# The codebook search of a four-layer kernel: one fp32 matmul per unit in place of three bf16 matmuls

## The reference

```
d = jnp.sum(z_flat ** 2, axis=1, keepdims=True) + jnp.sum(codebook ** 2, axis=1) - 2.0 * jnp.matmul(z_flat, codebook.T)
idx = jnp.argmin(d, axis=1)
z_q = codebook[idx]
```

## Time and profile before

| engine | busy us (share of the span) | instructions |
|---|---|---|
| TensorE, matmuls | 1207.6 (73%) | 5997 |
| TensorE, weight loads | 747.5 (45%) | 6040 |
| VectorE | 1359.2 (82%) | 1885 |
| ScalarE | 430.0 (26%) | 1354 |
| GpSimd | 1009.7 (61%) | 977 |

### The profile page before, as it was taken

How to read it: one execution, slowest core, us unless ns; L and a number is a source line. 1 busy time by engine, 2 the same in 40 slices (tenths; PEclk the granted TensorE clock), 3 DMA queues, 4 the chain that set the end, 5 groups by cost and what they waited for, 6 DMA issues and landing times. The chain is left out here.

```text
span 1657.5 us, 19707 instructions
## 1 busy us (share of the span) xinstructions
PE 1207.6 (73%) x5997; PEld 747.5 (45%) x6040; DVE 1359.2 (82%) x1885; ACT 430.0 (26%) x1354; POOL 1009.7 (61%) x977
## 2 busy tenths in 40 slices
PE   5889989698889987689857685676665566555554
PEld 2455555354444444244336454544444444444443
DVE  5568678789999999989967889987887777797775
ACT  1241000124333443243457231221112212111111
POOL 6158578444333443235777677777777777777772
PEclk9889999899999999789978797697777778767677
DMA  4051000012111121053476796787877878777773
GB/s 168 13 166 40 1 0 0 15 31 58 53 43 34 46 58 39 20 153 107 142 225 201 216 288 208 211 267 229 247 209 228 248 229 247 211 232 212 208 210 99
DMA packets 111101, 232.64 MB, mean 140 GB/s; under 512 B 14676, under 2 KB 60500, under 8 KB 110748
## 3 DMA queue, kind: packets, MB, share of 16 engines
q0 software_dynamic: 58176, 191.30, 39.0%
q1 hardware_dynamic: 52828, 40.17, 7.7%
HBM read 205.15 MB, written 26.26 MB: 140 GB/s over the span
## 5 line engine op out<-in xcount | busy, mean ns | idle before, releaser
L2076 POOL DMA_INDIRECT code_region<-corners,lead_region x252 | 240.9, 956 | 77.9 <-issue 75.8
L1864 DVE SCALAR_TENSOR_TENSOR max_region<-score,nc,max_region 128x512 f32<-128x512 f32 x324 | 230.5, 740 | 28.4 <-PE score L1433 26.2
L742 POOL TENSOR_TENSOR prod_acc<-prod_acc,prod_pool 128x752 f32<-128x752 f32 (+8 forms) x112 | 151.8, 1355 | 98.1 <-DVE prod_pool L715 90.6
L2076 POOL DMA_INDIRECT early_region<-corners,lead_region x136 | 129.0, 948 | 41.3 <-issue 40.8
L1458 PE MATMUL score<-ident,code_region 128*128 128x128 f32 x540 | 96.9, 340 | 77.6 <-DVE code_region L1913 73.0
L2076 POOL DMA_INDIRECT max_region<-corners,lead_region x130 | 124.1, 955 | 39.6 <-issue 38.7
L2076 POOL DMA_INDIRECT late_region<-corners,lead_region x126 | 119.9, 951 | 44.6 <-issue 37.8
L1864 DVE SCALAR_TENSOR_TENSOR max_region<-lead_score,nc,max_region 128x512 f32<-128x512 f32 x180 | 132.2, 741 | 8.1 <-PE lead_score L1433 7.6
L1458 PEld LDWEIGHTS score<-ident,code_region 128*128 128x128 f32 x540 | 78.6, 176 | 94.8 <-DVE code_region L1913 87.5
L1991 POOL DMA_INDIRECT late_region<-code_rows,block_id x35 | 37.0, 1058 | 135.3 <-DVE block_id L1706 98.7
L664 PE MATMUL y_ps<-prod_pe,w_scale 128*128 128x384 f32 (+9 forms) x396 | 107.6, 397 | 0.0
(11 more groups left out here) (289 smaller groups left out, 3098.2 us busy)
## 6 DMA issues: line engine op xcount, KB each, us to landing
corners<-lead_region SPq DMA_DIRECT2D x72, 192.0 KB
corners<-lead_region SPq DMA_DIRECT2D x8, 576.0 KB
code_rows<-codes_n SPq DMA_DIRECT2D x8, 516.0 KB, 4.2
codes_t<-in_codes_t SPq DMA_DIRECT2D x8, 512.0 KB, 3.7
codes_n<-in_codes SPq DMA_DIRECT2D x8, 512.0 KB, 4.4
code_region<-corners,lead_region POOLq DMA_INDIRECT x252, 3.7
x<-in_x SPq DMA_DIRECT2D x2, 1152.0 KB, 6.3
out<-x SPq DMA_DIRECT2D x4, 576.0 KB, 3.3
```

What stands on the lines that cost most here:

```text
L742: pool.tensor_tensor(to, to, v, ALU.add).then_inc(pooled, 1)
L1864: dve.scalar_tensor_tensor(r, score[SLOT[k]], nc2[:, m:m + 1], r, ALU.add, ALU.max).then_inc(dve_took, 1)
L2076: pool.indirect_dma_start(quad(T, k), None, table[j].rearrange("n s c -> n (s c)"), bass.IndirectOffsetOnAxis(index[j % B][:, at:at + 1], 0))\
```

## The change

The codes are loaded as they are into the 8192 words, with no slots, and no waits between the loads; POOL no longer works on them. z is kept in fp32 alone. A unit is one fp32 matmul. `code_views` gives the eight groups one after another.

```diff
         def _(pool):
             opening.pool(pool)
-            beside.pool(pool)
...
-                         Opening(tools, parts, x, xpad, gm32, moments, loads), CodeSplit(nc, tools, parts, a, ch, cl))
+                         Opening(tools, parts, x, xpad, gm32, moments, loads), CodeLoad(tools, parts, a, codes_t))
...
-        dve.sem_inc(self.affine, 1)
-        chain(dve.tensor_scalar(z, first, scale[:, 0:1], self.first_shift[:, 0:1], ALU.mult, ALU.add))
-        dve.wait_ge(self.high, 1)
-        dve.tensor_tensor(zl, z, zh, ALU.subtract).then_inc(self.low, 1)
+        dve.tensor_scalar(z, first, scale[:, 0:1], self.first_shift[:, 0:1], ALU.mult, ALU.add).then_inc(self.first, 1)
...
-        pe.wait_ge(self.high, 1)
-        pe.wait_ge(self.low, 1)
+        pe.wait_ge(self.first, 1)
...
-        act.wait_ge(self.affine, 1)
-        act.activation(zh, self.x[:, 0:self.FIRST], ACT.Identity, bias=self.first_shift[:, 0:1],
-                       scale=self.scale[:, 0:1]).then_inc(self.high, 1)
...
-        pool.wait_ge(self.high, 1)
+        pool.wait_ge(self.first, 1)
...
         for a, c, b in cuts:
-            z, zh, zl = places(a, c)
-            pool.tensor_scalar(z, x[:, a:c], self.scale[:, b:b + 1], self.shift[:, b:b + 1], ALU.mult, ALU.add)\
+            pool.tensor_scalar(places(a, c), x[:, a:c], self.scale[:, b:b + 1], self.shift[:, b:b + 1], ALU.mult, ALU.add)\
                 .then_inc(rest, 1)
-        pool.wait_ge(rest, 6)
-        for a, c, b in cuts:
-            z, zh, zl = places(a, c)
-            pool.tensor_copy(zh, z).then_inc(rest, 1)
-        pool.wait_ge(rest, 9)
-        for a, c, b in cuts:
-            z, zh, zl = places(a, c)
-            pool.tensor_tensor(zl, z, zh, ALU.subtract).then_inc(rest, 1)
-
-    DONE = 12
+    DONE = 6
...
+class CodeLoad:
+    def __init__(self, tools, ctx, a, codes):
+        self.a, self.codes = a, codes
+        self.loaded = tools.sem(ctx, "codes_t_loaded")
+
     def sp(self, sp):
         for g in range(GROUPS):
-            s = g % self.SLOTS
-            if g >= self.SLOTS:
-                sp.wait_ge(self.low, g - self.SLOTS + 1)
-            sp.dma_start(self.ct[:, s, :], self.a["codes_t"][:, g, :]).then_inc(self.ct_in[s], 16)
-
-    def pool(self, pool):
-        for g in range(GROUPS):
-            s = g % self.SLOTS
-            pool.wait_ge(self.ct_in[s], 16 * (g // self.SLOTS + 1))
-            pool.tensor_copy(self.ch[g], self.ct[:, s, :]).then_inc(self.high, 1)
-            pool.wait_ge(self.high, g + 1)
-            pool.tensor_tensor(self.cl[g], self.ct[:, s, :], self.ch[g], ALU.subtract).then_inc(self.low, 1)
+            sp.dma_start(self.codes[:, g, :], self.a["codes_t"][:, g, :]).then_inc(self.loaded, 16)
+        sp.wait_ge(self.loaded, 16 * GROUPS)
...
 def code_views(region):
-    high, low = [], []
...
-    return high, low
+    return region[:, 0:CODES].rearrange("p (g n) -> p g n", g=GROUPS)
...
-                    high, low_ = chunk_of(zh_early, zh_late, n), chunk_of(zl_early, zl_late, n)
-                    pe.matmul(o, ch[g][:, w], high, start=True, stop=False)
-                    pe.matmul(o, ch[g][:, w], low_, start=False, stop=False)
-                    pe.matmul(o, cl[g][:, w], high, start=False, stop=True).then_inc(score_ready, 1)
+                    pe.matmul(o, codes_t[:, g, w], chunk_of(z_early, z_late, n), start=True, stop=True)\
+                        .then_inc(score_ready, 1)
```

More of the change, by code:

```diff
@@ L777, in layer0 @@
                      (gb[:], a["gamma_beta"])]
[L778 removed]
+            codes_t, nc2, code_rows = codes
             with ExitStack() as parts:
                 guidance(nc, tools, xpad, w_guide, ident, ident_b[:], (sel_a, id3a), (sel_b, id3b), wta, wtb,
[L781 removed]
+                         Opening(tools, parts, x, xpad, gm32, moments, loads), CodeLoad(tools, parts, a, codes_t))
             with ExitStack() as parts:
@@ L818, in __init__ @@
         self.group_rooted = tools.sem(ctx, "x_group_rooted")
-        self.affine = tools.sem(ctx, "z_affine")
-        self.high = tools.sem(ctx, "first_high")
-        self.low = tools.sem(ctx, "first_low")
+        self.first = tools.sem(ctx, "first_ready")
         self.shifts = tools.sem(ctx, "z_shifts")
@@ L833, in dve_early, with dve @@
         chain(dve.tensor_tensor(var_x, qx, var_x, ALU.subtract))
-    def dve(self, dve, ps, each, z, zh, zl):
+    def dve(self, dve, ps, each, z):
         chain = Chain(dve, self.step)
@@ L1083, in finale @@
     region_code, region_lead, region_early, region_max, region_late = places
[L1084 to L1087, removed]
+    codes_t = code_views(region_code)
+    z_early = region_early[:, 0:PX * EARLY]
     x_flat = x.rearrange("p b n -> p (b n)")
@@ L1094, in z_places @@
         if c <= EARLY * PX:
-            return [v[:, a:c] for v in (z_early, zh_early, zl_early)]
-        return [v[:, a - EARLY * PX:c - EARLY * PX] for v in (z_late, zh_late, zl_late)]
+            return z_early[:, a:c]
+        return z_late[:, a - EARLY * PX:c - EARLY * PX]
     with ExitStack() as ctx:
@@ L1686, in _ @@
             act.sem_inc(y_saved, 1)
-            between.act(act, zh_early[:, 0:PX])
+            between.act(act)
             search_steps(step)
@@ L1969, in _ @@
             dve.sem_inc(pos_ready, 1)
-            between.dve(dve, gps[:, 0:2 * B], y0[:, 0:2 * CH], z_early[:, 0:PX], zh_early[:, 0:PX], zl_early[:, 0:PX])
+            between.dve(dve, gps[:, 0:2 * B], y0[:, 0:2 * CH], z_early[:, 0:PX])
             search_steps(step)
@@ L2169, in program @@
         code_rows = nc.dram_tensor("code_rows", [CODES // PER, PER * ROW], F32).ap()
-        ch, cl = code_views(code_region[:])
+        codes_t = code_views(code_region[:])
         y = lead_region[:, 0:N]
         between = Between(tools, ctx, x.rearrange("p b n -> p (b n)"), y, stats, xy, moments, gb, gm32)
-        layer0(nc, tools, a, x, xpad, gm32, gm8, ident, (ch, cl, nc2, code_rows), y, stats, xy, moments, gb, between)
+        layer0(nc, tools, a, x, xpad, gm32, gm8, ident, (codes_t, nc2, code_rows), y, stats, xy, moments, gb, between)
         early_region = tools.sb(ctx, "early_region", [P, 5120])
```

10 lines of the change are left out of this document (1 added, 9 removed).

## The result

The changed kernel takes 1738.94 us, the median of 4 runs (1734.21 to 1739.90); the kernel before, beside it on the same chip, 1658.30. The ratio is 1.048, 95% interval [1.0468, 1.0493]. The profiled execution took 1738.93 us, with a span of 1737.1 us, 79.6 more than before. The forecast was 1733 (1712 to 1757).

What follows compares the result with a forecast made beforehand. TensorE was taken as the bound in all chunks but 6, which VectorE sets. 83.5 for the search - 6.5 - 1.0 - 1.7 = +74.3 us on 1659.3, less 1.3 to the runs' median, gave 1733 us (1712 to 1757).

Steps and rivals of the forecast that it cites:

- guidance: Stage before the search: without POOL's code splits, TensorE's first softmax wait and slow work behind it go; -6.5 us (-3.8 to -8).
- between the layers, to ScalarE's first unit: Before the search: TensorE starts on z itself, not on the result of VectorE's subtraction; -1.0 us.
- chunks 1 to 5: Codebook search: TensorE's 59.3 us plus 1.2 us of remaining wait make 60.5 per chunk, +9.4 each, +47 us for five.
- chunk 6: Search chunk with depthwise taps: TensorE leads until unit 10 of the first step, then VectorE's unchanged work; +3.5 us (0 to 13.5).
- chunk 7: Search chunk where the norm chain holds TensorE in the first step; four steps estimated together at +9 us (3 to 13.5).
- chunk 8: Last search chunk: TensorE is the bound except in step 1; +10.5 us (7 to 13.5).
- behind the search, to POOL's stream: End of search: POOL's gathers hang on the find at unit 7, so start less late than the search ends; -1.7 us (-4 to 0).
- from there to the end: From POOL's stream of gathers to the kernel's end: no change predicted, 0.
- The price of a unit: Search on TensorE: one fp32 matmul is two passes, 0.858 us instead of 0.647, 0.211 us more per unit.
- the first (less shows, +40 to +52): Rival, chance 0.07: VectorE's own work fills chunks 7 and 8 and step 1's slack holds; 1700 to 1711 us.
- The second: Rival, chance 0.05: fp32 matmul costs two bf16 matmuls, 0.432 us per unit, so VectorE sets each chunk; -34, 1626 us.
- the third: Rival, chance 0.06: weight loads or the clock show, 0.2 to 0.4 us more per unit; 1850 to 1960 us, partly from 1757.

## Why the prediction was right

| term | predicted | measured |
|---|---|---|
| guidance | -6.5 | -6.15 (branches begin at 79.29, before at 85.44) |
| between the layers, to ScalarE's first unit | -1.0 | -0.3 |
| chunk 0 | +13.5 | +14.0 |
| chunks 1 to 5 | +47 | +48.9 (60.88 against 51.1) |
| chunk 6 | +3.5 | +2.4 |
| chunk 7 | +9 | +7.8 |
| chunk 8 | +10.5 | +11.6 |
| behind the search, to POOL's stream | -1.7 | -2.3 |
| from there to the end | 0 | +3.7 |
| sum | +74.3 | +79.6 |

**The price of a unit** was read off and the earlier trace rows, from another fp32 matmul in the same kernel: two passes per call, each as long per column as two bf16 matmuls. It came out at 0.86 us, as predicted, and the run with four bf16 matmuls, with chunks of the same length, shows that TensorE pays for nothing else there.

**Who sets the pace.** TensorE in chunks 0 to 5, with little left of the waits for VectorE's find pairs in step 1. Here the count of VectorE's work between two uses of a bank was what mattered: 0.211 us times 64 units would have been 13.5 a chunk, and 9.8 came. TensorE's own work is the 59.3 us worked out (steps 0 and 3 with three turns 15.05 each, steps 1 and 2 with two 14.61 each); the rest, 1.56 us where 1.2 was predicted, lies at the unit named, unit 0 of step 2, and at the two pairs behind it:

```profile
642.55 2.78 PE L1389 MATMUL score<-late_region,code_region 128*128 128x512 f32 x6
646.44 1.99 PE L1389 MATMUL lead_score<-late_region,code_region 128*128 128x512 f32 x4 [1.11 <-DVE max_region L1821]
648.29 1.98 PE L1389 MATMUL score<-late_region,code_region 128*128 128x512 f32 x4
```

Three units from 642.55 would end at 645.12, the next begins at 646.44 (1.3 us); it and the three behind it take 1.85 and 1.83 us a pair instead of 1.72. The trace before has five such waits around this step in chunk 5 (586.72 to 598.47), not four, and the last two stand at units 0 and 2 of step 2, so the 5.3 us were not all in step 1.

**Chunks 6 to 8** came out near their sums, in part by luck. VectorE does set chunk 6: it is busy for 71.8 us of it (71.6 before). But the first step grew by 2.8 us where 2.1 was worked out, the next two by 1.2 and 1.0, and the last shrank by 2.6 (18.70 against 21.31), which the prediction doesn't have. With 256 columns the same chunk grew by only 0.8 (76.65 us), as its step 1 lost less to TensorE's lower clock level (last section). The steps of chunk 7 grew by 2.4, 2.5, 1.1 and 1.9 where 2.5, 1.6, 3.1 and 1.8 were estimated, those of chunk 8 by 3.4, 2.2, 3.1 and 2.9 where 3.4, 2, 1.7 and 3.4 were.

**Guidance.** The wait, the slow convolution behind it and the slow transposes went, as worked out, and all of it belongs to POOL's splitting: the run with the splits spread has the bf16 search and gained 6.3 us on the whole time. How well the size of this term was hit says little: where the splits stayed as they were, the branches begin at 83.19 us (four bf16 matmuls), 85.44 (before) and 85.66 (two).

**Between the layers** TensorE did start on z, 0.9 us earlier against the branches' start, but its first units are slow (TensorE in order of time, and the stage table of the first two units):

```profile
311.95 3.78 PE L1389 MATMUL lead_score<-early_region,code_region 128*128 128x512 f32 x4 [2.98 <-DVE early_region L882]
315.52 2.44 PE L1389 MATMUL score<-early_region,code_region 128*128 128x512 f32 x4
```

```profile
311.95:315.52 3.57, 3.57 (x4) 1.51 (x5) 0.01 (x1) 0.69 (x1) 3.02 (x2) 0.50 0.01 2
```

The first two units take 3.57 us (311.95 to 315.52), 1.79 each, twice 0.858 and a little more, at a granted clock of 0.50: this is the lower level, 1.2 GHz, behind a wait of 2.98 us. The kernel before starts at this level too (its first matmuls are 0.43 us apart, 319.82 to 320.25), but a unit is 1.28 us there. So the longer unit makes this start dearer: from TensorE's first unit to ScalarE's it is 2.1 us instead of some 1.5 (the trace before lacks the record of the first matmul; its start is put one spacing ahead of the second, at 318.97), which ate 0.6 here, and the first step of chunk 0 grew by 3.83 us where 16 x 0.211 = 3.4 would have been the price, which is the 0.5 by which chunk 0 missed. The term itself is small beside its spread: from the branches' start to ScalarE's first unit it is 232.4 to 235.6 us in the six kernels with bf16 matmuls.

**The largest miss** is the part of "behind the search" that should have stayed as it was: 3.7 us, of which 3.3 come behind the gather that waits over 6 us for TensorE (at 1004.19 us; before, at 927.87). The gathers that POOL issues show 953 to 963 ns on average where they showed 948 to 956; over 644 of them that is the 3.6 us by which their busy times differ:

```profile
L2033 POOL DMA_INDIRECT code_region<-corners,lead_region x252 | 242.3, 961 | 77.8 <-issue 74.6
```

In the other kernels of this study this group stands at 956 to 962 with bf16 and at 961 to 967 with fp32 in the search. From the gather that waits to the end, the six kernels with bf16 matmuls take 729.2 to 730.3 us and the four with fp32 731.4 to 733.0, in one profile each; the kernel with four bf16 matmuls, whose search is as long, takes 730.2. So the miss goes with the fp32 kernels and not with the length of the search, but what in them makes it stays open.

The rivals: the first (less shows, +40 to +52) fell since chunks 7 and 8 did grow, by 7.8 and 11.6. The second fell on its premise alone, the third on the 0.86 us of a unit and on the runs with narrower matmuls.

## What to carry to other kernels

An fp32 matmul of 512 columns costs TensorE here what four bf16 matmuls of its width cost, so three bf16 products are cheaper by a quarter (0.647 against 0.858 us), and what replaces them could be priced by an fp32 matmul that the trace already held. The gain of a faster unit and the loss of a slower one differ when two engines run close together: count the second engine's work between two uses of the same buffer before multiplying the difference by the number of units. Of a change with a good and a bad part, the good one (no splits beside the softmax: 6 us) could be had alone here, by moving the work to where its neighbour waits.

## What the runs showed that was not expected

A short wait of TensorE can cost more than its length, and not always the same. In chunk 6, step 1, TensorE waits some 2.2 us before the depthwise weights (L220) in each kernel (2.27 in the changed one, 2.21 with 256 columns); the two send the same columns through TensorE there, the second in twice as many calls. The changed kernel, TensorE in order of time; then the stage table from 702 to 708 us and of the whole step:

```profile
701.14 2.88 PE L220 MATMUL lead_score<-pooled,wk 128*128 128x1 f32 x18 [2.27 <-DVEq L240]
...
705.73 1.92 PE L1389 MATMUL lead_score<-late_region,code_region 128*128 128x512 f32 x2
707.44 1.89 PE L1389 MATMUL score<-late_region,code_region 128*128 128x512 f32 x2
```

```profile
702.00:704.00 2.00, 2.00 (x13) 2.00 (x12) 2.00 (x3) 0.99 (x1) 0.00 (x0) 0.59 0.03 8
704.00:706.00 2.00, 2.00 (x4) 0.97 (x4) 1.58 (x3) 0.00 (x0) 1.84 (x3) 0.50 0.33 33
706.00:708.00 2.00, 2.00 (x3) 0.74 (x3) 1.04 (x2) 0.00 (x0) 1.57 (x1) 0.50 0.61 231
...
693.83:716.34 22.51, 20.25 (x59) 10.43 (x58) 19.89 (x38) 7.42 (x23) 7.39 (x7) 0.85 0.17 48
```

With 256 columns, from 704 to 708 us and the same step:

```profile
704.00:706.00 2.00, 2.00 (x6) 1.60 (x5) 1.90 (x4) 0.00 (x0) 1.85 (x3) 0.50 0.32 43
706.00:708.00 2.00, 2.00 (x10) 1.68 (x10) 2.00 (x4) 0.12 (x1) 1.29 (x2) 0.77 0.57 221
...
693.53:714.39 20.86, 18.65 (x92) 16.10 (x91) 19.80 (x38) 7.42 (x22) 7.41 (x7) 0.92 0.17 51
```

At a granted clock of 0.50, the 1.2 GHz level, units follow each other at 1.71 us (705.73 to 707.44). The changed kernel is at this level until 708, the other leaves it earlier (0.77 from 706 to 708), and the step of the first is 1.65 us longer. The calls need not be the reason: with four bf16 matmuls this step is 20.86 us too, with 128 columns 22.63. A wait of 1.19 us in guidance was followed by a convolution of 7.67 instead of 6.03 us, while the 1.3 us in each chunk of the search cost nothing behind them (granted clock 1.00 in steps 1 and 2 above). What decides when the lower level comes and how long it lasts, these runs don't show. Here it moved one step by 1.65 us, which is the size of most differences left in the table; whether it made the others isn't shown.
